# A transformer block on one core: input sums at other steps, a new order of the tail, and dense products of two batches from high and low parts

## The reference

```
mod = (silu(c) @ wmod).reshape(4, 6, 1, -1)          # sa, ca, ga, sb, cb, gb
h = layernorm(x) * (1 + ca) + sa
q, k, v = h @ wq + bq, h @ wk + bk, h @ wv + bv      # weights = codes * block scales; 16 heads of 128
attn = softmax(q @ k.T / sqrt(128)) @ v
x = x + ga * (attn @ wo + bo)
h = layernorm(x) * (1 + cb) + sb
out = h @ W.T                                        # the dense product, W is 256 x 256
top 2 of 8 experts by softmax(h @ gate_w.T); lora = sum over them of weight * (h @ A.T) @ B.T
x = x + gb * (out + lora)
```

## Times and profile before

| what | value |
|---|---|
| median of 3 runs | 762.7 us (762.2 to 763.58) |
| profiled execution, its own time | 762.64 us |
| its span (first to last instruction) | 760.5 us |
| busy: PE, DVE, ACT, POOL | 750.6, 653.3, 563.1, 626.8 us (99%, 86%, 74%, 82%) |
| granted clock of TensorE | 1.00 of full speed |
| matmul records | 4128 |

### The profile page before, as it was taken

One profiled execution on the slowest core, in us unless ns is written; L12 is line 12 of the kernel. 1 busy time (PEld: TensorE's weight loads), 2 busy tenths in 40 slices (PEclk: granted clock), 3 DMA queues, 4 the chain that ended last, 5 costly groups with the idle time before them and its releaser, 6 DMA issues.

```text
span 760.5 us, 15086 instructions
## 1 busy us (share of the span) xinstructions
PE 750.6 (99%) x4128; PEld 650.3 (86%) x4128; DVE 653.3 (86%) x1267; ACT 563.1 (74%) x1226; POOL 626.8 (82%) x655
## 2 busy tenths in 40 slices
PE   8999999999999999999999999999999999999988
PEld 7888888888888888888888888888888888888877
DVE  7899989889798888889798888889798888889776
ACT  4787787877877778777777778777777787778741
POOL 5488899899797888879798888879788788989852
PEclk9999999999999999999999999999999999999999
DMA  8354344444455344553455344553455345655203
GB/s 266 91 152 123 88 101 135 130 121 97 112 138 159 91 105 119 155 131 93 102 148 157 92 105 119 154 131 96 103 148 156 91 104 138 167 138 133 50 1 111
DMA packets 71725, 92.20 MB, mean 121 GB/s; under 512 B 19477, under 2 KB 36598, under 8 KB 71670
## 3 DMA queue, kind: packets, MB, share of 16 engines
q1 hardware_dynamic: 52368, 73.21, 37.5%
q10 hardware_dynamic: 19302, 18.42, 8.1%
HBM read 23.39 MB, written 2.11 MB: 34 GB/s over the span
## 4 chain that ended last, share of the span: by engine, by line
PE 87%; POOL 5%; DVE 5%; issue 1%; ACT 1%; ACTq 0%; POOLq 0%; DVEq 0%
PE score L1630 14%; PE score L1631 14%; PE score L1632 14%; PE o L1630 7%; PE o L1632 7%; PE o L1631 7%; PE qv L1630 3%; PE qv L1631 3%; PE qv L1632 3%; PE ky L1630 3%; PE ky L1631 2%; PE ky L1632 2%; POOL pT_parts L594 2%; PE y L1905 2%; PE y L1901 2%; PE y L1900 2%
## 5 line engine op out<-in xcount | busy, mean ns | idle before, releaser
L594 POOL TENSOR_TENSOR pT_parts<-pT,pT_hi 128x512 fp32r<-128x512 f32 x224 | 286.3, 1304 | 50.4 <-ACT pT_hi L849 48.2
L918 ACT ACTIVATE prob<-score,neg_max 128x512 f32<-128x512 f32 x256 | 173.2, 687 | 74.9 <-DVE neg_max L1398 74.8
L1413 DVE STREAM_TRANSPOSE pB<-prob 128x512 f32<-128x512 f32 x252 | 161.9, 690 | 17.0 <-PE o L1632 10.3
L1398 DVE TENSOR_REDUCE neg_max<-score 128x1 f32<-128x512 f32 x256 | 159.3, 683 | 0.4 <-PE score L1632 0.2
L849 ACT ACTIVATE pT_hi<-pT 128x512 fp32r<-128x512 f32 x224 | 129.8, 624 | 4.9 <-DMA pT<-pB 4.1
L1630 PE MATMUL score<-k_hi,q_hi 128*128 128x512 f32 x256 | 101.4, 396 | 0.2 <-DVE q_lo L1285 0.2
L1631 PE MATMUL score<-k_lo,q_hi 128*128 128x512 f32 x256 | 100.4, 392 | 0.0
L1632 PE MATMUL score<-k_hi,q_lo 128*128 128x512 f32 x256 | 99.8, 390 | 0.0
L1630 PE MATMUL o<-pT_hi,v_hi 128*128 128x512 f32 x248 | 97.0, 391 | 0.4 <-POOL pT_parts L594 0.4
L1632 PE MATMUL o<-pT_hi,v_lo 128*128 128x512 f32 x248 | 96.6, 390 | 0.0
L1631 PE MATMUL o<-pT_parts,v_hi 128*128 128x512 f32 x248 | 96.6, 389 | 0.0
(11 more groups left out here) (466 smaller groups left out, 2040.8 us busy)
## 6 DMA issues: line engine op xcount, KB each, us to landing
pT<-pB SPq DMA_DIRECT2D x1008, 64.0 KB, 2.0
x_nat<-in_L_attn_x_dram ACTq DMA_DIRECT2D x4, 512.0 KB, 4.9
out_dram<-x_nat SPq DMA_DIRECT2D x8, 256.0 KB, 2.2
stage<-in_L_attn_wv_codes_dram ACTq DMA_DIRECT2D x7, 256.0 KB
stage<-in_L_attn_wv_scales_dram ACTq DMA_DIRECT2D x14, 128.0 KB
stage<-in_L_attn_wq_codes_dram ACTq DMA_DIRECT2D x7, 256.0 KB
stage<-in_L_attn_wq_scales_dram ACTq DMA_DIRECT2D x14, 128.0 KB
stage<-in_L_attn_wk_codes_dram ACTq DMA_DIRECT2D x7, 256.0 KB
```

What stands on the lines that cost most here:

```text
L594: pool.tensor_tensor(turned_quarter(par, i, pT_lo), turned_quarter(par, i), quarter(pT_hi, i).bitcast(f32), ALU.subtract).then_inc(p_lo_ok, 1)
L918: act.activation(prob[:, i], score_ps[i][:, :], ACT.Exp, bias=neg_max[:, i:i + 1], accum_out=row_sum[:, s % 2, i:i + 1]).then_inc(exp_ok, 1)
L1398: dve.tensor_reduce(neg_max[:, i:i + 1], score_ps[i][:, :], AX.X, ALU.max, negate=True).then_inc(max_ok, 1)
L1413: dve.transpose(pB[:, s % 2, :, :, i].rearrange("p g k q -> p k g q"), prob[:, i].rearrange("p (k g q) -> p k g q", k=QT, g=G)).then_inc(p ...
```

## The change

What it does:

- Of the four input sums for pb = 1, VectorE now makes sum 3 in step 6 of the first pair (before: end of step 1 of pair 1), sum 2 in step 3 of pair 1 before `q_lo` (before: end of step 2), sum 4 in step 4 after the maxima (before: end of step 3). ScalarE's casts and GpSimd's remainders follow, at the steps that the diff shows. A third table, `T_HIGH`, counts the casts apart from the remainders.
- In the tail, VectorE makes the last additions to y before it waits for batch 2, and ScalarE normalises batch 3 instead of VectorE. GpSimd's `times_gb` and `add_gated_bo(3)` stand elsewhere.
- The dense products of batches 1 and 3 are made by `three`, from high and low parts of the input and of `w_gb`. ScalarE writes the high parts (over `hT_hi`, `w_hi`), GpSimd the low parts (over `hT_lo`, `w_lo`).

```diff
+        FAST = (1, 3)
+        fast_in = {b: tuple(v[:, c, 0:DC * S].rearrange("p (c s) -> p c s", c=DC) for v in (hT_hi, hT_lo)) for b, c in ((1, 1), (3, 0))}
+        fast_w = {b: (w_hi[m], w_lo[m]) for b, m in ((1, "q"), (3, "k"))}
...
+        T_HIGH = {(0, 1): 1, (0, 2): 2, (0, 4): 3, (0, 3): 4, (1, 1): 5, (1, 3): 6, (1, 2): 7, (1, 4): 8}
+        T_DONE = {(0, 1): 1, (0, 2): 2, (0, 4): 3, (0, 3): 4, (1, 2): 5, (1, 3): 6, (1, 4): 7, (1, 1): 8}
...
 (GpSimd, pair)
                     if s % 4 in (1, 2):
                         for m in "qk":
                             mixed_low(m, u3 if s % 4 == 1 else u2, mixed)
-                    if last and s == 5:
-                        times_gb(0)
-                    if not (last and s == SPP - 1):
+                    if isinstance(p, int) and p == 1 and s == 3:
+                        prob_low(n - 1, 0, range(1))
+                        product("k", p + 1)
+                        prob_low(n - 1, 0, range(1, 2))
+                        input_mix_lo(1, 2)
+                        prob_low(n - 1, 0, range(2, 4))
+                    elif not (last and s == SPP - 1):
                         prob_low(n - 1, (s - 1) % 2)
...
 (GpSimd, tail)
             attended(1)
+            times_gb(0)
+            add_gated_bo(3)
+            inverse_std(B + 1)
             times_gb(1)
-            inverse_std(B + 1)
-            add_gated_bo(3)
+
+            def fast_weights_low(b):
+                pool.wait_ge(fast_hi, fast_count(b, 1))
+                pool.tensor_tensor(fast_w[b][1][:, :, :], w_gb[b], fast_w[b][0][:, :, :].bitcast(f32), ALU.subtract).then_inc(fast_ok, 1)
...
             gate(2)
             attended(2)
+            fast_weights_low(1)
+            times_gb(2)
             inverse_std(B + 2)
-            pool.wait_ge(x1_ok, B)
-            times_gb(2)
+            fast_input_low(1)
             inverse_std(B + 3)
             times_gb(3)
+            fast_weights_low(3)
+            fast_input_low(3)
...
 (ScalarE, first_cycle_step, pair; tail)
+                if isinstance(p, int) and p == 1 and s == 3:
+                    input_mix_hi(1, 2)
...
+                        if isinstance(p, int) and p == 1 and s == 4:
+                            input_mix_hi(1, 4)
...
             o_high(N, q_hi)
+            fast_weights_high(1)
             ffn_input_high(1)
+            fast_input_high(1)
             ffn_normalise(2)
             lora_out(1)
             ffn_input_high(2)
+            ffn_normalise(3)
+            fast_weights_high(3)
             lora_out(2)
             ffn_input_high(3)
+            fast_input_high(3)
             odds(0)
             lora_out(3)
...
 (VectorE, tail)
+            dve.wait_ge(y_ok, QT * (N - 1))
+            y_add(N - 1, B - 1, 2, False, y_end)
             dve.wait_ge(x1_ok, 3)
             statistics(2)
-            y_add(N - 1, B - 1, 2, False, y_end)
             gate(B - 1)
             attended(B - 1)
             statistics(B - 1)
-            dve.wait_ge(z2_tr, DC * 2)
-            normalise(2 * B - 1)
             router(0)
...
 (TensorE, dense)
+                if b in FAST:
+                    pe.wait_ge(fast_ok, fast_count(b, 1 + DC))
                 for k in tiles or range(2 * half, 2 * half + 2):
                     for c in range(DC):
+                        cut = (slice(None), c, slice(k * P, (k + 1) * P))
+                        if b in FAST:
+                            ins = three(f_tile(b, k), tuple(v[cut] for v in fast_in[b]), tuple(w[:, c] for w in fast_w[b]),
+                                        c == 0 and k % 2 == 0, False)
```

More of the change, by code:

```diff
@@ L253, in bass_adaln_mxfp4_attention_moe_lora_kernel @@
         dense_mm, neg_ok = sem("dense_mm"), sem("neg_ok")
-        xb_ok = [sem(f"xb_ok{b}") for b in range(B)]
+        xb_ok = sem("xb_ok")
         bias_ok = sem("bias_ok")
@@ L270, in bass_adaln_mxfp4_attention_moe_lora_kernel @@
         y_mm, y_ok = sem("y_mm"), sem("y_ok")
-        yg_ok = [sem(f"yg_ok{b}") for b in range(B)]
+        yg_ok = sem("yg_ok")
         x1_ok, z2_tr, z2_ev = (sem(n) for n in ("x1_ok", "z2_tr", "z2_ev"))
@@ L328, in first_half, with fast_count @@
             return 1 + "kq".index(m)
+        def fast_count(b, part):
+            return (1 + DC) * FAST.index(b) + part
         def tokens(b):
@@ L589, in input_mix_lo, with prob_low @@
                 pool.tensor_tensor(t_lo(pb, i), t_sum(pb, i), t_hi(pb, i).bitcast(f32), ALU.subtract).then_inc(t_ok, 1)
-            def prob_low(n, par):
-                for i in range(4):
+            def prob_low(n, par, quarters=range(4)):
+                for i in quarters:
                     pool.wait_ge(p_hi_ok, 4 * n + i + 1)
@@ L627, in add_gated_bo @@
                 pool.tensor_tensor(x_nat[:, b * QT:(b + 1) * QT], x_nat[:, b * QT:(b + 1) * QT],
-                                   ga_bo[:, 1:2].to_broadcast([P, QT, D]), ALU.add).then_inc(xb_ok[b], 1)
+                                   ga_bo[:, 1:2].to_broadcast([P, QT, D]), ALU.add).then_inc(xb_ok, 1)
             def times_gb(b):
@@ L717, in pair @@
                         if isinstance(p, int) and p == 1:
+                            input_mix_lo(1, 3)
+                        block_sums("q", p + 1)
+                        if isinstance(p, int) and p == 1:
                             input_mix_lo(1, 4)
-                        block_sums("q", p + 1)
                         block_sums("k", p + 1)
+                        if isinstance(p, int) and p == 1:
+                            input_mix_lo(1, 1)
                     elif s == 6:
@@ L1099, in pair @@
                         act.dma_start(gb_row[:, :], bass.AP(gate_dram.tensor, D, [[0, P], [2 * D, B], [1, D]])).then_inc(ld_gb, 16)
-                    if isinstance(p, int) and p == 1 and s < 4:
-                        for i in ((), (1,), (2,), (3, 4))[s]:
-                            input_mix_hi(1, i)
+                    if isinstance(p, int) and p == 1 and s in (1, 2):
+                        input_mix_hi(1, (1, 3)[s - 1])
                     if s == SPP - 2 and not last:
@@ L1144, in ffn_input_high, with fast_weights_high, fast_input_high @@
                     ffn_input_out(b, c, (qv_ps, ky_ps)[c])
+            def fast_weights_high(b):
+                act.wait_ge(wg_ok[b], 1)
+                act.activation(fast_w[b][0][:, :, :], w_gb[b], ACT.Copy).then_inc(fast_hi, 1)
+            def fast_input_high(b):
+                for c in range(DC):
+                    act.wait_ge(z2_ev, DC * b + c + 1)
+                    act.activation(fast_in[b][0][:, c], h2T[b][:, c], ACT.Copy).then_inc(fast_hi, 1)
             o_high_last(N - 1)
@@ L1501, in pair @@
                         maximum(n, i)
+                    if isinstance(p, int) and p == 1 and s == 4:
+                        input_mix(1, 4)
                     if last and s == SPP - 1:
@@ L1530, in pair @@
                             row_statistics(0, i)
+                    if isinstance(p, int) and p == 1 and s == 3:
+                        input_mix(1, 2)
                     if t == 0:
@@ L1848, in dense @@
                 pe.wait_ge(wg_ok[b], 2)
+                if b in FAST:
+                    pe.wait_ge(fast_ok, fast_count(b, 1 + DC))
                 for k in tiles or range(2 * half, 2 * half + 2):
                     for c in range(DC):
-                        ins = pe.matmul(f_tile(b, k), h2T[b][:, c, k * P:(k + 1) * P], w_gb[b][:, c],
-                                        start=(c == 0 and k % 2 == 0), stop=False)
+                        cut = (slice(None), c, slice(k * P, (k + 1) * P))
+                        if b in FAST:
+                            ins = three(f_tile(b, k), tuple(v[cut] for v in fast_in[b]), tuple(w[:, c] for w in fast_w[b]),
+                                        c == 0 and k % 2 == 0, False)
+                        else:
+                            ins = pe.matmul(f_tile(b, k), h2T[b][cut], w_gb[b][:, c], start=(c == 0 and k % 2 == 0), stop=False)
                 ins.then_inc(dense_mm, 1)
```

46 lines of the change are left out of this document (21 added, 25 removed).

## The result

The changed kernel takes 768.23 us (median of 6 runs, 767.69 to 768.84), the kernel before 762.87 in the same comparison: ratio 1.007, interval 1.0058 to 1.0081. It is slower by 5.4 us. Its profiled execution took 768.09, with a span of 766.3 and a mean granted clock of 0.993, where before it was 760.5 and 1.00.

The account below looks back on a forecast made before the run. TensorE, 87% of the span, was taken as the bound. First pair +0.6, second -1.0, last -0.35 and tail +5.3 gave +4.5 on 762.6 us: 767.1 predicted, range 763.0 to 770.2.

Parts of the forecast that it names:

- Tail, up to the wait: Tail before batch 1's dense product: GpSimd's low parts ready at 734.65, TensorE wants them at 729.76, waits 5.0 us.
- The turns at the gate: Tail: VectorE's gate and sum of batch 3 alternate with GpSimd's operations, 2.35 us; sign: gate L1375 over 1.5 us.
- the third rival: Tail: TensorE's pace falls in the 5 us wait, 1.2 to 3.0 us lost, time 769.1; chance 0.20.
- Tail, the router: Tail: VectorE's router for batches 0 to 2 caught behind three GpSimd operations of 1.26, margin at 747.65 instead of 745.0.
- TensorE's work, -1.2: Tail: each half of batch 1's and 3's dense products takes 1.43 instead of 1.73 us; four halves save 1.2.
- First pair, +0.6: Step 6, first pair: VectorE's sum (1,3) before `q_lo`, `k_lo` delays TensorE's next scores 0.6 us (+0.3 to +1.5).
- Second pair, -1.0: Second pair of heads: TensorE waits of 2.50 go, GpSimd's late remainders cost 1.5; net -1.0 us (-1.9 to 0).
- The stretch that I named: Second pair, TensorE's output product of step 0 to that of step 5; 55.29 us before, to shorten by 0.5 to 1.5.
- Last pair, -0.35: Last pair: batch 0's weights times gate leave step 5, TensorE's wait for quarters goes; -0.35 us (0 to -0.4).
- Rival 1: Tail slips less without VectorE and GpSimd taking turns: 764.8 without the gate's, 762.6 without the router's too; chance 0.22.
- rival 2: Tail: low parts ready in time because GpSimd has idle time there; faster, 759.2 us; chance 0.08.
- rival 4: Second pair: GpSimd's backlog costs all of the 2.50 saved; 768.1 us; chance 0.50 together with the main forecast.

Follow-up runs that it names:

- the kernel with the wait filled: Changed kernel plus nine fp32 matmuls on TensorE in its wait before batch 1's dense product, their output overwritten; 765.85 us, ratio 1.0042.
- the fp32 version: Changed kernel with all four dense products in fp32, no high and low parts made, all else the same; 761.94 us, ratio 0.9988.
- the middle alone: Kernel before with only the input sums moved to their new steps, no other part of the change; 763.14 us, ratio 1.0002.
- batch 1's parts alone: Changed kernel with only batch 1's dense product made from high and low parts, batch 3's in fp32; 765.45 us, ratio 1.0032.
- batch 3's parts alone: Changed kernel with only batch 3's dense product made from high and low parts, batch 1's in fp32; 762.97 us, ratio 0.9998.

## Why the prediction was right, and where not

**Direction and size.** Forecast 767.1, measured 768.23: slower, for the reason given, that GpSimd can't have the low parts ready. That the sum (+4.5, measured +5.4) came out so near is in part luck, since errors went against each other: the pace of TensorE (+1.9 in the tail), which I had kept out as a rival, and a second pair that won 0.7 less than I said, against an end of the tail that I had made about 1.1 too long and a first pair 0.3 too dear.

**Tail, up to the wait: right.** Taken from the same instruction of the last heads, the forecast's times were met within 0.3: GpSimd's sum of batch 2 (725.1, came at 725.3), the inverse deviation (732.15, came at 731.9), the low parts (734.65, came at 734.3). TensorE waited 4.56 where I had 5.0. The turns at the gate exist but fell mostly on GpSimd: its two operations took 2.0 longer, VectorE's gate 1.21, not the "over 1.5" that I had named as its sign; its sum took 1.63. What I had priced at 2.35 is there as about 2.0, at another engine. The exclusive lock of the Trainium skill (SBUF — State Buffer, Who interferes with whom) fits both; the trace agrees, with 1.78 for an operation of 0.7.

**Tail, the pace: the third rival came in.** I gave it 0.20 and 2 us. It cost 1.87 in the tail, 2.4 by the medians. The forecast had the wait and its length, and the earlier trace rows showed half pace where TensorE came from a time without work; the step that failed is taking the 1.43 of full pace for a half behind a wait longer than any in the trace before. The one that I leaned on, 1.8 us, said nothing about one of 4.6.

**Tail, the router: mis-sized.** I had it "caught behind three GpSimd operations of 1.26", from 745.0 to 747.65, +2.65. It was caught three times, but for less (0.47, 1.33 and 0.92 instead of 0.26 each): from its start to its margin it takes 5.14 instead of 3.19, +1.95, in each kernel with batch 3's parts, and 3.20 in those without. In the kernel with the wait filled the tail is +4.23 against my +5.3; the router is 0.7 of the difference, earlier transposes of batch 3 (0.3) most of the rest.

**TensorE's work, -1.2:** the halves of batch 3's product take 1.5 (747.87 to 749.37), near the 1.43 forecast. No gain from it shows at the end, though no kernel has the cheaper matmuls without the parts' other costs: the fp32 version, with more work for TensorE, has a shorter tail (46.53) than any version with parts (48.63 at best).

**First pair, +0.6: wrong cause.** It was +0.28, and not from the sum before `q_lo` and `k_lo`: the sum takes 0.68, VectorE then idles 0.61 before `k_lo`, waiting for ScalarE and behind it TensorE. "There VectorE never idles" was read off the old order, in which two sums of 1.77 each had pushed it back. In the new one they slip in between GpSimd's operations:

```profile
84.64 0.67 DVE L1361 TENSOR_TENSOR x_nat<-u,x_nat 128x512 f32<-128x512 f32 x1
85.24 0.68 DVE L1361 TENSOR_TENSOR z<-router_space,y_acc 128x512 f32<-128x512 f32 x1
```

and GpSimd's four remainders take 6.15 instead of 5.95. TensorE loses 0.2 on their quarters (89.3 to 90.0). That the loss of 0.25 stays when the sum is moved away clears the sum; that the turns cause it fits the rows, but was not tried by itself.

**Second pair, -1.0: right at product 4, wrong behind it.** TensorE waits 0.76 for the remainder of sum 4, and its restart costs 0.16; I had 1.5 with the turn. The profile calls this wait "issue", but GpSimd's remainder ends at 161.19 and TensorE starts at 161.29:

```profile
159.92 1.27 POOL L600 TENSOR_TENSOR gb_row_parts<-gb_row,gb_row_parts 128x512 fp32r<-128x512 f32 x1
...
161.29 0.48 PE L1678 MATMUL qv<-gb_row_parts,wq_hi 128*128 128x512 f32 x1 [0.76 <-issue]
```

The stretch that I named is 0.84 shorter (forecast 0.5 to 1.5). The step that failed is "so it is not paid twice": the backlog goes on, and another 0.50 is paid in small restarts from the scores of step 6 on. The pair wins 0.34.

**Last pair, -0.35:** -0.44. **Rival 1** (no turns) is out, and so is **rival 2** (lows in time); **rival 4**, a second pair that wins nothing, was nearer than the forecast's -1.0, and the middle alone shows it: no change.

## What to carry to other kernels

Splitting a product into three cheaper ones saved TensorE 0.6 us for each batch (at full clock) and needed six more operations for each (three casts, three low parts) on engines that had no time just then; ask first what makes the parts, and when. A wait of TensorE that grows by some microseconds may be paid twice, as time and as pace behind it, and filling it with matmuls that nobody needs was worth 2.4 us. When an operation of one engine is moved away from a stall, count the load of the engine that has to follow it: reordering GpSimd's queue only moved the wait, giving one of its operations to an idle VectorE took most of it away (0.27 of 0.69 was left).

## What the runs showed of the hardware that was not expected

- TensorE's granted clock fell to 0.50 during a wait of 4.56 us (and again with batch 1's parts alone, 4.57 us) and stayed there for 4.3 us of work (about 3 in the other). In the profiled waits of 3.17 and 1.8 it stayed at 1.00. A long wait is not the only thing it falls behind: in the changed kernel and in the one with batch 3's parts alone it was 0.50 to 0.59 for some microseconds about 12 to 15 us into the kernel, with no wait of TensorE longer than 0.7 us since its first one, and it was 1.00 there in the kernel before; why is open. At the start of the kernel the pace was half while the clock was given as 1.00, so the spacing of matmuls is the surer sign.
- Turns between VectorE and GpSimd hit even tiny operations: GpSimd's 128x4 multiplication took 1.18 us (changed kernel) and 1.12 us (fp32 version) instead of 0.20 beside a VectorE operation of 1024 elements.
- A phase of 0.1 us seems to decide who pays for them. In the first pair two VectorE sums took 1.77 each in the kernel before and 0.67 in the changed one, with the same four GpSimd operations beside them, which took 5.95 and 6.15. The first sum starts 1.32 us behind the first of the four before (84.07 and 82.75) and 1.22 behind it after (84.64 and 83.42), and one of the four takes 1.26: the one time it comes just after the second has begun, the other time just before. The phase was not varied by itself.
